# Gated cross-attention and a binarized feed-forward on one core: the second layer norm's statistics of tiles 10 to 31 move from VectorE to ScalarE, and all orders are planned anew

## The reference

```python
def _L0_xattn_ref(query, key):
    a = jnp.einsum('bqd,bkd->bqk', query, key)
    e = jax.nn.softmax(a, axis=-1)
    return jnp.einsum('bqk,bkd->bqd', e, key)
def _L0_ffn_ref(x, weight_real, bias):
    alpha = jnp.mean(jnp.abs(weight_real), axis=1, keepdims=True)
    return jnp.einsum('bsi,oi->bso', x, alpha * jnp.sign(weight_real)) + bias
x = x + jnp.tanh(g_xattn[0]) * _L0_xattn_ref(_layernorm(x), ctx_4096)
x = x + jnp.tanh(g_ffn[0]) * _L0_ffn_ref(_layernorm(x), weight_real, bias)
```

## Time and profile before

| | |
|---|---|
| median of 3 runs | 985.3 us (984.62 to 986.54) |
| profiled execution: time | 985.79 us |
| profiled execution: span, first to last instruction | 984.0 us |
| mean granted TensorE clock in it | 0.988 |
| PE busy | 934.0 us, 95% |
| DVE busy | 840.8 us, 85% |
| ACT busy | 589.3 us, 60% |
| POOL busy | 134.9 us, 14% |
| chain that ended last: PE, DVE, ACT | 69%, 10%, 5% |

### The profile page before, as it was taken

One profiled execution on the slowest core, in us unless ns is written; L12 is line 12 of the kernel. 1 busy time (PEld: TensorE's weight loads), 2 busy tenths in 40 slices (PEclk: granted clock), 3 DMA queues, 4 the chain that ended last, 5 costly groups with the idle time before them and its releaser, 6 DMA issues.

```text
span 984.0 us, 14349 instructions
## 1 busy us (share of the span) xinstructions
PE 934.0 (95%) x5201; PEld 462.9 (47%) x5201; DVE 840.8 (85%) x1197; ACT 589.3 (60%) x655; POOL 134.9 (14%) x262
## 2 busy tenths in 40 slices
PE   1669999999999999999999999999999999999998
PEld 1445554444444444454444444444444445444443
DVE  6587799897888989899989979998989888889864
ACT  5999973856587573646657364745667464562320
POOL 0011020131001110203111220201102020111000
PEclk9779999999999999999999999999999999999999
DMA  9589747696897988787995959967797967765374
GB/s 332 181 233 229 225 128 199 179 202 112 185 218 154 217 158 221 150 177 168 217 239 97 242 121 237 196 144 202 165 230 125 240 137 152 196 128 102 65 177 186
DMA packets 365141, 178.66 MB, mean 182 GB/s; under 512 B 353424, under 2 KB 353424, under 8 KB 354448
## 3 DMA queue, kind: packets, MB, share of 16 engines
q1 hardware_dynamic: 365072, 177.76, 76.9%
HBM read 55.58 MB, written 33.55 MB: 91 GB/s over the span
## 4 chain that ended last, share of the span: by engine, by line
PE 69%; DVE 10%; issue 7%; ACT 5%; POOL 2%; DMA 2%; SPq 0%; ACTq 0%; DVEq 0%; POOLq 0%
PE y_ps L2621 53%; PE y_ps L2589 7%; PE c_ps L2569 5%; PE s_ps L2553 4%; DVE natural L1571 3%; ACT xn_q L952 1%; DVE xr L1656 1%; DMA xr<-in_x_dram 1%; ACT natural L933 1%; DMA ring_a<-natural 1%; ACT spare L1063 1%; DVE st L1661 1%; DVE snap_a L1689 0%; ACT xn_q L919 0%; DVE xr L1790 0%
## 5 line engine op out<-in xcount | busy, mean ns | idle before, releaser
L2621 PE MATMUL y_ps<-wsign,ring_a 128*128 128x512 fp8e4 x1792 | 400.6, 379 | 2.3 <-DMA ring_a<-natural 1.5
L2621 PEld LDWEIGHTS y_ps<-wsign,ring_a 128*128 128x128 f16 x1792 | 173.9, 98 | 209.8 <-DMA ring_a<-natural 2.8
L2621 PE MATMUL y_ps<-spare,ring_a 128*128 128x512 fp8e4 x896 | 202.8, 379 | 0.7 <-ACT snap_b L1087 0.7
L933 ACT ACTIVATE natural<-xn_a 128x1024 f16<-128x1024 f32 x76 | 79.5, 1053 | 109.2 <-DVE xn_a L1803 49.9
L2621 PEld LDWEIGHTS y_ps<-spare,ring_a 128*128 128x128 f16 x896 | 87.3, 98 | 105.8 <-issue 1.5
L952 ACT ACTIVATE xn_q<-xr,nm,r 128x1024 f32<-128x1024 f32 x62 | 76.8, 1238 | 68.7 <-POOL nm L791 34.3
L1571 DVE TENSOR_TENSOR natural<-xn_a,natural 128x1024 f16<-128x1024 f32 x78 | 94.7, 1216 | 10.9 <-ACT natural L933 10.9
L1571 DVE TENSOR_TENSOR natural<-xn_q,natural 128x1024 f16<-128x1024 f32 x64 | 78.1, 1220 | 25.3 <-ACT natural L933 25.0
L2621 PE MATMUL y_ps<-sg,ring_a 128*128 128x512 fp8e4 x448 | 99.4, 379 | 0.0
L1656 DVE SCALAR_TENSOR_TENSOR xr<-c_ps,coef,xr 128x512 f32<-128x512 f32 x104 | 77.6, 746 | 21.5 <-PE c_ps L2569 21.1
L2569 PE MATMUL c_ps<-kd,pt 128*128 128x512 f16 x256 | 79.7, 394 | 11.5 <-DVE xr L1656 8.6
(11 more groups left out here) (121 smaller groups left out, 1001.4 us busy)
## 6 DMA issues: line engine op xcount, KB each, us to landing
xr<-in_x_dram SPq DMA_DIRECT2D x32, 1024.0 KB, 6.2
out_dram<-xr SPq DMA_DIRECT2D x30, 1024.0 KB, 5.1
spare<-n_L_ffn_weight_real_dram SPq DMA_DIRECT2D x8, 1024.0 KB, 7.3
ctx_f<-in_ctx_dram SPq DMA_DIRECT2D x8, 512.0 KB, 6.6
xr<-n_L_ffn_weight_real_dram SPq DMA_DIRECT2D x4, 1024.0 KB, 5.0
ctx_f<-n_L_ffn_weight_real_dram SPq DMA_DIRECT2D x4, 1024.0 KB, 7.3
out_dram<-xr SPq DMA_DIRECT2D x8, 256.0 KB, 2.2
ring_a<-natural SPq DMA_TRANSPOSE x102, 4.5
```

What stands on the lines that cost most here:

```text
L933: nc.scalar.activation(natural[:, i % RN, 0, :], src, ACT.Copy).then_inc(high_set, 1)
L2621: last = nc.tensor.matmul(y_ps[:, BANKS[j] + n, :], ring_a[:, slot_a(p, j), part, k, :], RIGHT[j][:, k // 2, chunk(n), k % 2], start=(firs ...
```

## The change

`LN2_ACT` becomes `range(4,32)`: for tiles 10 to 31 the `bn_stats` and `bn_aggr` of DVE go, the addition sums what it writes, and ACT runs `square_rows2`. POOL's `scale2` follows with one instruction less (it needs no sign change of the mean). All lists are planned anew, `NAT` and the first tiles' lists too, though nothing about tiles 0 to 9 is different in kind. No helper changes. In the changed kernel the lines behind ACT's list stand 22 lines later (L1571 is L1593 there, L1651 is L1673).

```diff
-        LN2_ACT = range(4,10)
+        LN2_ACT = range(4,32)
...
             load_x(0)
             load_keys(0)
+            load_gates()
             load_w(0)
+            load_x(1)
             load_w(1)
-            load_gates()
-            load_x(1)
+            load_w(2)
             load_x(2)
...
-            copy_third(2, 0)
-            normalise2(10)
+            square_rows2(10)
```

More of the change, by code:

```diff
@@ L1144, in _ @@
             high_x1(2, 0)
+            direct_high_q(4, 1)
             copy_pt(3)
-            direct_high_q(4, 1)
+            sign(8)
+            high_x1(2, 1)
+            sign(9)
             sum_abs(7)
-            high_x1(2, 1)
-            sign(8)
-            sign(9)
+            sign(10)
+            take_w(4)
             sum_abs(8)
-            take_w(4)
-            sign(10)
+            sum_abs(9)
             exp(4)
-            sum_abs(9)
             sign(11)
             sum_abs(10)
+            sign(12)
             copy_pt(4)
-            sign(12)
             take_w(5)
@@ L1232, in _ @@
             direct_high_q(10, 0)
+            direct_high_q(10, 1)
             copy_third(1, 0)
+            exp(9)
             copy_first(1, 1)
-            exp(9)
-            direct_high_q(10, 1)
+            square_rows2(8)
+            copy_pt(9)
+            copy_third(1, 1)
+            snapshot(1, 0)
             high_a(1, "A22")
-            copy_pt(9)
-            snapshot(1, 0)
-            square_rows2(8)
             sum_rows1(11)
@@ L1271, in _ @@
             high_a(2, "S4")
+            square_rows1(13)
+            copy_third(2, 0)
+            normalise2(10)
+            copy_third(2, 1)
             snapshot(2, 1)
-            copy_third(2, 1)
-            square_rows1(13)
+            square_rows2(11)
+            exp(12)
             direct_high_q(13, 0)
@@ L1277, in _ @@
             normalise2(11)
-            exp(12)
             high_a(3, "A11")
+            copy_pt(12)
             high_a(3, "A12")
-            copy_pt(12)
             high_a(3, "S3")
+            high_a(3, "S2")
+            high_a(3, "S1")
+            sum_rows1(14)
+            copy_first(3, 0)
             exp(13)
-            high_a(3, "S2")
-            copy_first(3, 0)
-            sum_rows1(14)
-            high_a(3, "S1")
+            square_rows2(12)
+            copy_pt(13)
             high_a(3, "A22")
             square_rows1(14)
-            copy_pt(13)
+            normalise2(12)
             direct_high_q(14, 0)
+            copy_first(3, 1)
             direct_high_q(14, 1)
-            copy_first(3, 1)
+            snapshot(3, 0)
+            high_a(3, "S4")
             copy_third(3, 0)
-            normalise2(12)
-            snapshot(3, 0)
             sum_rows1(15)
             snapshot(3, 1)
-            high_a(3, "S4")
             square_rows1(15)
+            square_rows2(13)
             copy_third(3, 1)
@@ L1310, in _ @@
             high_a(4, "S1")
+            copy_first(4, 0)
+            sum_rows1(16)
+            exp(15)
             high_a(4, "S2")
-            copy_first(4, 0)
-            exp(15)
-            high_a(4, "S4")
-            copy_pt(15)
-            sum_rows1(16)
-            high_a(4, "A22")
             copy_first(4, 1)
             square_rows1(16)
+            copy_pt(15)
+            square_rows2(14)
+            high_a(4, "A22")
             direct_high_q(16, 0)
-            normalise2(14)
-            snapshot(4, 0)
-            high_keys(2)
-            snapshot(4, 1)
             direct_high_q(16, 1)
             copy_third(4, 0)
+            high_a(4, "S4")
+            high_keys(2)
+            snapshot(4, 0)
+            normalise2(14)
+            snapshot(4, 1)
+            square_rows2(15)
+            copy_third(4, 1)
             normalise2(15)
             high_a(5, "A11")
+            sum_rows1(17)
             high_a(5, "A12")
-            copy_third(4, 1)
-            sum_rows1(17)
             square_rows1(17)
@@ L1418, in _ @@
             high_a(8, "S3")
+            high_a(8, "S2")
             high_a(8, "A22")
-            high_a(8, "S2")
+            exp(23)
+            high_a(8, "S1")
             copy_first(8, 0)
-            exp(23)
             copy_pt(23)
-            high_a(8, "S1")
             sum_rows1(24)
+            square_rows2(22)
             square_rows1(24)
             copy_first(8, 1)
+            high_a(8, "S4")
             direct_high_q(24, 0)
@@ L1462, in _ @@
             square_rows1(27)
+            high_a(9, "S4")
             copy_third(9, 1)
-            high_a(9, "S4")
+            direct_high_q(27, 0)
             normalise2(24)
-            direct_high_q(27, 0)
+            square_rows2(25)
+            exp(26)
+            direct_high_q(27, 1)
             normalise2(25)
-            exp(26)
             high_a(10, "A11")
-            direct_high_q(27, 1)
+            copy_pt(26)
             high_a(10, "A12")
-            copy_pt(26)
             high_a(10, "S3")
@@ L2337, in _ @@
             low_q(26, 1)
+            low_a(9, "A22")
             attention(25, 0)
-            low_a(9, "A22")
             attention(25, 1)
+            finish_pair(9, "C11", 1)
             attention(25, 2)
+            low_a(9, "S4")
+            attention(25, 3)
+            low_q(27, 0)
             finish_pair(9, "C22", 0)
-            attention(25, 3)
-            low_a(9, "S4")
             max_logits(26)
+            split_probs(26)
             finish_pair(9, "C22", 1)
-            low_q(27, 0)
+            low_q(27, 1)
             finish_pair(9, "C21", 0)
@@ L2350, in _ @@
             finish_pair(9, "C21", 1)
-            low_q(27, 1)
+            finish_pair(9, "C12", 0)
             make_s3(10)
-            split_probs(26)
-            finish_pair(9, "C12", 0)
+            attention(26, 0)
             low_a(10, "A12")
@@ L2370, in _ @@
             low_a(10, "S1")
+            attention(26, 2)
+            attention(26, 3)
+            finish_pair(10, "C11", 0)
+            low_q(28, 0)
+            low_q(28, 1)
             attention(27, 0)
@@ L2419, in _ @@
             finish_pair(11, "C22", 1)
+            low_a(12, "A11")
             finish_pair(11, "C21", 0)
-            low_a(12, "A11")
             make_s3(12)
             finish_pair(11, "C21", 1)
+            add_bias(28)
+            finish_pair(11, "C12", 0)
             low_a(12, "A12")
-            finish_pair(11, "C12", 0)
-            finish_pair(11, "C12", 1)
             low_q(31, 0)
```

1134 lines of the change are left out of this document (569 added, 565 removed), and 32 rows, old and new, of the table NAT.

## The result

The changed kernel takes 991.4 us (median of 3 runs, 991.11 to 991.48) against 985.3: a ratio of 1.0059, 95% interval 1.0039 to 1.0078. It is slower by about 6 us, where 983.1 us and a range from 979.5 to 988.0 were forecast. The profiled execution has a span of 989.6 us (984.0 before).

What follows compares the result with a forecast made beforehand. PE was taken to be at its pace (216 ns a matmul), so only its waits could be won. 985.8 + 0.2 - 3.2 + 1.0 = 983.8 us for the profiled execution, 983.1 us expected for the median, range 979.5 to 988.0.

Steps and rivals of the forecast that it cites:

- ACT's waits: PE's waits ended by ACT, whose list gets heavier: 1.0 us more, bounds 0 and 4 us.
- the chain from `square_rows2` to A11 and its slack: Chain to a pair's first block: 13.7 us for pair 6 against 16.5 us of PE work, 2.8 us slack.
- more than 2 us in sum behind 300 us: Sign of being wrong: PE waits ended by ACT (normalise2 to A11, snapshot, copy_first) above that sum.
- The late start: First plain_block 2.6 us later, at 74.2 us; absorbed in PE's existing waits before pair 1 except 0.2 us.
- the two marks that I gave for it: A11 of pair 1: near 261 us if right, at 263 us or later if wrong.
- DVE's waits: PE's waits ended by DVE, 4.0 us behind 262 us: 3.2 us gone, bounds 0 and 4.0 us.
- The three that I named: PE's waits of 1.61, 0.86 and 0.46 us for additions in DVE's list, taken as gone.
- Busy times: Whole span: DVE from 841 to about 774 us, ACT from 589 to 645 us, neither showing in the time.
- the end has no new wait: End: the last 304 matmuls run without a wait; the last two tiles' longer chain has 7 us of slack.
- ACT is waited for: Rival: A11 chains slip 2.53 us beyond their slack in two tight pairs, 987.3 us; chance 0.10.
- late start stays: Rival: A11 of pair 1 moves with the 2.6 us late first plain_block, 985.7 or 987.9 us; chance 0.12.

Runs made afterwards that it cites:

- run 2: Changed kernel with four calls of ACT's list (two snapshot, two copy_pt) moved ahead: 988.2 us, ratio 1.0024 to the kernel before.
- run 4: Changed kernel, but square_rows2 of tiles 10 to 31 squares only 512 of 2048 columns: 990.2 us, ratio 1.005 to the kernel before.
- run 9: Changed kernel, order untouched, with 17 added matmuls whose result nobody reads, up to the first plain_block: 989.2 us, ratio 1.0034 to the kernel before.
- run 7: Changed kernel with the start of the kernel before, four ACT calls and two DVE calls moved ahead: 984.4 us, ratio 0.9992 to the kernel before.
- run 12: The kernel of run 7 with two more ACT calls, then five more ACT and DVE calls moved ahead: 981.7 us, ratio 0.9955 to the kernel before.
- run 6: Kernel before from pair 0 on, with every list and NAT beginning in the changed kernel's orders: ratio 1.0028 to the kernel before.
- run 1: Changed kernel with one ACT call moved, sign(6) behind take_x1(0, 1): 989.8 us, ratio 1.0043 to the kernel before.
- run 8: Changed kernel with one place of the start put back on PE, DVE and ACT: 990.4 us, ratio 1.005 to the kernel before.

## Why the prediction was wrong

The sum came to 983.1 us and 991.4 was measured; of the 8.3 us between them these steps hold 7.7 (4.3, 2.5 and 0.9).

*ACT's waits* is the step that failed first: 1.0 us more than before was forecast, with bounds 0 and 4, and 5.3 more came (5.7 for 0.33). I priced the chain from `square_rows2` to A11 and its slack, and there I was right: no A11 block waits more than 0.31 us for its data, and none for ACT (the 0.42 and 0.39 us at two pair starts are waits for DVE's `finish_pair` of the pair before). The waits arose at `snapshot` (3.4 us) and `copy_pt` (2.3). For the first I had named a mark ("more than 2 us in sum behind 300 us", which is what happened) but no price of its own; the second I had not named. I treated ACT as a load with two thirds of the span. It is a queue with one buffer, `xn_q`, that it shares with DVE, and what counts is what stands behind `direct_high_q(u, 1)`. Runs 2 and 4 show that.

*The late start.* I walked the lists to a first `plain_block` at 74.2 us (72.86 measured) and let all but 0.2 us be absorbed ahead of pair 1. Run 9 bears out the absorption of the lateness alone. But I counted only when PE starts, not how fast it runs then: the thin stretch that I had written down step by step is what the clock fell in. Slow matmuls on top of the lateness cost some 2.5 us by run 9 that no term held, though I had used the slower pace for `scores(2)` just ahead. Pair 1's block then came at 262.73 us, between the two marks that I gave for it.

*DVE's waits.* 3.2 us forecast as gone, 2.3 gone (4.0 to 1.7). The three that I named went; one of 0.91 us came at 517.70 of the very kind that I took to be planned away, an addition behind `low_q` that waits for ACT's half row (DVE stood idle for 2.60 us ahead of it).

*Busy times.* DVE came to 780 us for 774, ACT to 638 for 645. The summing addition isn't free (below): I had counted its read in the chain to A11 and forgot it in DVE's sum. And `square_rows2` is busy for 2.2 us (49 us by 22), not for its pitch of 2.53.

*Right:* neither the 61 us taken off DVE nor the 49 us put on ACT are in the time as such (runs 4, 7 and 12), and the end has no new wait: the last 320 matmuls run without one. Of the rivals, "ACT is waited for" came nearest, by another mechanism than the one I gave it, and "late start stays" held for its size, not for its reason; that both could come together was left out of the range.

## What to carry to other kernels

When work moves to an engine with room, list on that engine each instruction that another engine's pace depends on, and look at what stands ahead of it that waits for a third party: the price is there, not in the busy share. Where an order is planned anew, compare PE's thin stretches as well as its start times, because matmuls behind a thin stretch can run at the lower clock (here sixteen took 5.83 us in place of 3.5). And a slower result of a re-planned kernel says little about the edit until the two are taken apart: half-and-half orders and a few moved calls showed here that the loss of 6 us came from the orders, and that a kernel with the edit can be 4 us faster than the one before.

## What was not expected of the hardware

The summing addition is followed by an instruction that reads the sum out, 83 ns each, which the plain one doesn't have; 88 new ones are 7.3 us of DVE. From the groups of the changed kernel (busy us, mean ns, idle before):

```profile
L1673 DVE DVE_READ_ACCUMULATOR xr<-c_ps,coef,xr 128x1 f32 x112 | 9.3, 83 | 0.0
```

The clock fell in a stretch in which PE was never idle for more than 2.10 us at once, and 17 matmuls put into it kept it at 1.00. With the new start the executions differ more than with the old one: in run 6 three at a mean granted clock of 0.989 to 0.991 took 985.3 to 986.6 us, eight at 0.983 or 0.984 took 987.9 to 990.8; the kernel before, on that chip, was at 0.987 or more in each of its counted executions. Runs 1 and 8 split in the same way. The traces show how the two differ, though only two of them are of the faster sort: in those of runs 1 and 6 the clock was full already during `scores(2)` (1.95 us), and the first block came at 70.50 and 71.02 us; in the changed kernel's and in those of runs 2 and 4 `scores(2)` took 2.87 to 3.62 us, and the block came at 72.86 to 73.97. In all five the clock fell afterwards. The three timed executions of the changed kernel itself don't split by their clock (991.1 to 991.5 us at 0.986 and 0.990), and what decides in which of the two ways the start runs stays open.
